# Row-loaded, TensorE-transposed second sequence, joint h transposes and a reordered last sequence in a LayerNorm–FFN kernel

## Chip, cores and metric

One Trainium2 chip, one core. The time is that of one execution on the device, in microseconds.

## What is computed

Eight sequences `b`, each `x[b]` of 256 x 1024 floats with a weight matrix of its own, chosen by `ids[b]`; then a feed-forward network that all share:

```python
y = x[b] @ weight[ids[b]].T                      # 1024 x 1024, fp32
h = layernorm(y) * gamma + beta
a = gelu(fake_quant(h) @ fake_quant(w1).T + b1)  # int8 grid, one scale per row
out[b] = x[b] + fake_quant(a) @ fake_quant(w3).T + b3
```

## The kernel before

Every engine has a program written out by hand; they meet only in semaphores, and each engine and each DMA queue works strictly in its order. All loads and stores are issued by SP.

**One sequence** is two token tiles (t = 0, 1) of 128. Its fp32 product is made from parts: x and weight are transposed, ScalarE (ACT) copies each transposed tile from PSUM as the high part (`split_first`, `split_w`, `split_x`), VectorE (DVE) subtracts to get the low part (`low_first`, `low_w`; GpSimd (POOL) does `low_x`), and TensorE (PE) adds hi·hi, hi·lo and lo·hi. The product has four units (output half kh times contraction half ch) of two pieces; `piece(b, u, k)` is 12 matmuls of 512 columns (L1011 to L1038). The first sequence is loaded on 128 partitions and transposed on PE against an identity, 8 fp32 transposes of 128x128 per step, in the order of the list `FIRST` (`transpose_first`, L1088). Sequences 1 to 7 are loaded in four DMAs of 32 partitions each (`load_unit`, L264; `load_x`, L277) and transposed on DVE in 32x32 blocks (`transpose_w`, L756; `transpose_x`, L772).

**The network** per sequence: ACT copies y (`copy_y`), DVE takes statistics, POOL makes the normalisers and applies gamma and beta (`scale_and_shift`, L417), DVE finds the row scale, ACT rounds (`round_h`), PE transposes h (`transpose_h`, L1047), ACT takes it (`take_h`, L571), PE multiplies by w1 (`ffn1`), DVE rescales (`rescale1`), POOL adds b1, ACT takes Gelu, and the same with w3 (`ffn2`); ACT scales (`scale_ffn2`) and POOL finishes (`finish`, L425): one multiplication by a row of scales and the addition of x + b3. Both h tiles pass through the same PSUM bank, so that the second transpose waits for `rescale1` of the first tile:

```python
if t == 1:
    pe.wait_ge(ffn1_scaled, KH * (TT * f + 1))
...
transpose_tile(h_r[:, t, :], f_ps[:, 0], h_transposed)
```

w1 and w3 come as 16 row tiles; each is loaded (`load_prep`), maxed on DVE (`max_prep`), scaled in four groups (`scales_prep`), rounded on POOL (`round_prep`), transposed on PE (`prepare`) and taken by ACT (`take_prep`), all of it between the pieces of the first two sequences. Two of the slots they are loaded into first hold gamma and beta; `load_prep` of tile 4 or 5 therefore waits until POOL has broadcast these rows (`rows_ready`, L316).

**The order.** After the start (L1206 to L1253 on PE) a loop runs five times (`period(p)`, p = 2 to 6): the FFN of sequence p-1 lies between the pieces of p and p+1. SP's loop (L334) ends with

```python
store(p - 1, 0)
load_unit(p + 2, 1)
store(p - 1, 1)
```

so the load of a unit stands behind a store that waits for POOL's `finish(p-1, 0)`. POOL's loop (L455) is low_x, add_b1, residual (both tiles of x + b3), normalisers, low_x, add_b1, four gamma and beta steps, then `finish` of both tiles. The last sequence has code of its own (`last_period`): DVE takes part of gamma and beta (L875), the FFNs of the last two sequences are woven by hand, and POOL adds b3 to the last x (L506).

## Time and profile before

| | us |
|---|---|
| median of 3 runs (lowest, highest) | 389.77 (389.49, 391.45) |
| the profiled execution | 390.59 |
| its span | 388.7 |
| PE busy | 336.1 (86%) |
| DVE busy | 287.2 (74%) |
| POOL busy | 278.2 (72%) |
| ACT busy | 230.0 (59%) |

PE's busy share is a mean over three stretches: the start to about 131 us, the loop to about 330 us, and the end. A matmul's shown duration is longer than its distance to the next, because matmuls are pipelined; distances between starts are what counts.

### The profile page before, as it was taken

Reading aid. Unit: us, or ns where it says so; the run is one execution under the profiler, and the core shown is the slowest. Engines: PE = TensorE matmul, PEld = TensorE weight load, DVE = VectorE, ACT = ScalarE, POOL = GpSimd, SP = SyncE. Lnnn points to the kernel's source line nnn. Section 1 sums busy time; section 2 is a strip of 40 time slices with the busy share of each in tenths; the row PEclk is TensorE's granted clock in tenths of the full one; section 3 lists DMA queues with packets and bytes.
Section 4 is the critical chain, followed back from the end, with each engine's and each line's share of the span. In section 5 each row is a group of like instructions: output and inputs, shape, how many; then the busy total and the mean of one; then the engine's idle time right before and its main releaser. Section 6 shows DMA issues by size and latency. Waiting matters only on the chain.

```text
span 388.7 us, 5553 instructions
## 1 busy us (share of the span) xinstructions
PE 336.1 (86%) x1732; PEld 227.5 (59%) x1760; DVE 287.2 (74%) x345; ACT 230.0 (59%) x241; POOL 278.2 (72%) x170
## 2 busy tenths in 40 slices
PE   2998816898788999999999999998999999997591
PEld 2786604666565666656665666565656666853240
DVE  1388539766797987788868886888688868388635
ACT  2244519653698747774777567756874777336460
POOL 1404329648559859995999599958996899778563
PEclk9999965999899999999999999999999999999897
DMA  7999998559549799829981999099909900440014
GB/s 251 369 259 332 188 203 197 147 113 208 164 100 217 180 272 219 160 75 293 222 166 57 286 220 192 37 291 217 208 3 287 235 18 0 160 166 1 0 56 162
DMA packets 49946, 67.33 MB, mean 173 GB/s; under 512 B 3078, under 2 KB 43014, under 8 KB 49930
## 3 DMA queue, kind: packets, MB, share of 16 engines
q1 hardware_dynamic: 49930, 67.14, 70.2%
q8 instruction: 8, 0.13, 0.1%
q14 instruction: 8, 0.07, 0.1%
HBM read 58.74 MB, written 8.39 MB: 173 GB/s over the span
## 4 chain that ended last, share of the span: by engine, by line
POOL 38%; issue 16%; PE 8%; DVE 6%; ACT 2%; POOLq 0%; ACTq 0%
POOL x_lo L446 7%; POOL y L421 7%; POOL o L429 6%; POOL x_res L437 6%; POOL a L441 4%; POOL y L423 4%; POOL o L432 3%; PE f_ps L1069 3%; PE t_ps L1069 1%; POOL rstd L407 1%; PE a_ps L1018 1%; DVE x_t L929 1%; PE a_ps L1019 1%; PE a_ps L1020 1%; DVE y L881 1%
## 5 line engine op out<-in xcount | busy, mean ns | idle before, releaser
L1018 PE MATMUL a_ps<-w_hi,x_hi 128*128 128x512 f32 x256 | 109.6, 428 | 2.0 <-ACT y L552 1.2
L1020 PE MATMUL a_ps<-w_hi,x_lo 128*128 128x512 f32 x256 | 101.8, 398 | 0.0
L1019 PE MATMUL a_ps<-w_lo,x_hi 128*128 128x512 f32 x256 | 101.8, 398 | 0.0
L1069 PE MATMUL f_ps<-w_q,q_t 128*128 128x512 bf16 x375 | 88.8, 380 | 5.7 <-ACT q_t L586 3.1
L763 DVE STREAM_TRANSPOSE t_ps<-w_nat 128x1024 f32<-128x1024 f32 x56 | 67.5, 1239 | 20.9 <-DMA w_nat<-in_L_cond_weight 20.6
L537 ACT ACTIVATE w_hi<-t_ps 128x1024 fp32r<-128x1024 f32 x56 | 57.2, 1023 | 31.4 <-DVE t_ps L763 30.3
L769 DVE TENSOR_TENSOR w_lo<-t_ps,w_hi 128x1024 fp32r<-128x1024 f32 x56 | 66.8, 1217 | 9.5 <-ACT w_hi L537 9.3
L1069 PEld LDWEIGHTS f_ps<-w_q,q_t 128*128 128x128 bf16 x400 | 37.1, 98 | 52.4 <-ACT q_t L586 6.4
L1018 PEld LDWEIGHTS a_ps<-w_hi,x_hi 128*128 128x128 f32 x256 | 49.6, 194 | 15.9 <-ACT y L552 3.1
L1020 PEld LDWEIGHTS a_ps<-w_hi,x_lo 128*128 128x128 f32 x256 | 49.2, 192 | 11.2
L1019 PEld LDWEIGHTS a_ps<-w_lo,x_hi 128*128 128x128 f32 x256 | 49.6, 194 | 9.1
L446 POOL TENSOR_TENSOR x_lo<-x_t,x_hi 128x1024 fp32r<-128x1024 f32 x14 | 33.6, 2401 | 22.1 <-ACT x_hi L543 21.9
L441 POOL TENSOR_TENSOR a<-a,rows 128x1024 f32<-128x1024 f32 x14 | 34.5, 2461 | 15.1 <-DVE a L836 15.0
L429 POOL TENSOR_TENSOR o<-o,w_scale_row 128x1024 f32<-128x1024 f32 x14 | 33.3, 2377 | 11.1 <-ACT o L591 11.1
L437 POOL TENSOR_TENSOR x_res<-x_res,rows 128x1024 f32<-128x1024 f32 x14 | 33.8, 2434 | 3.9 <-DMA x_res<-in_x 3.9
L432 POOL TENSOR_TENSOR o<-o,x_res 128x1024 f32<-128x1024 f32 x14 | 33.7, 2409 | 1.1
L423 POOL TENSOR_TENSOR y<-y,rows 128x1024 f32<-128x1024 f32 x12 | 28.7, 2396 | 0.9
L421 POOL TENSOR_TENSOR y<-y,rows 128x1024 f32<-128x1024 f32 x12 | 28.6, 2380 | 0.0
L812 DVE TENSOR_REDUCE g_max<-a 128x1 f32<-128x1024 f32 x14 | 17.0, 1213 | 13.0 <-ACT a L577 13.0
L581 ACT ACTIVATE a<-a,magic,g_inv 128x1024 f32<-128x1024 f32 x14 | 17.4, 1243 | 12.2 <-DVE g_inv L800 12.2
L804 DVE TENSOR_REDUCE h_max<-y 128x1 f32<-128x1024 f32 x14 | 17.0, 1217 | 9.3 <-POOL y L423 9.3
L543 ACT ACTIVATE x_hi<-x_t 128x1024 fp32r<-128x1024 f32 x14 | 14.7, 1052 | 15.2 <-DVE x_t L778 13.4
(143 smaller groups left out, 456.1 us busy)
## 6 DMA issues: line engine op xcount, KB each, us to landing
w_nat<-in_L_cond_weight SPq DMA_DIRECT2D x112, 256.0 KB, 6.6
x_nat<-in_x SPq DMA_DIRECT2D x28, 256.0 KB, 9.9
x_res<-in_x SPq DMA_DIRECT2D x7, 1024.0 KB, 7.0
out<-o SPq DMA_DIRECT2D x14, 512.0 KB, 2.9
w_nat<-in_L_cond_weight SPq DMA_DIRECT2D x4, 512.0 KB, 7.0
w_q<-in_L_ffn_w SPq DMA_DIRECT2D x4, 512.0 KB, 9.1
w_scale_row<-in_L_ffn_w SPq DMA_DIRECT2D x3, 512.0 KB, 13.4
o<-in_x SPq DMA_DIRECT2D x2, 512.0 KB, 4.5
```

What stands on the lines that cost most here:

```text
L421: pool.tensor_tensor(row, row, gamma_row, ALU.mult).then_inc(gamma_done, 1)
L429: pool.tensor_tensor(o[:, t, :], o[:, t, :], w_scale_row[:, 1, :], ALU.mult).then_inc(out_scaled, 1)
L437: pool.tensor_tensor(x_res[:, t, :], x_res[:, t, :], b3_row, ALU.add).then_inc(x_b3_ready, 1)
L441: pool.tensor_tensor(a[:, t, :], a[:, t, :], b1_row, ALU.add).then_inc(ffn1_biased, 1)
L446: pool.tensor_tensor(x_lo[:, half], x_t[:, half], x_hi[:, half].bitcast(F32), ALU.subtract).then_inc(x_lo_ready, 1)
L537: act.activation(part_of_unit(w_hi, u, k), piece_bank(k), ACT.Copy).then_inc(w_hi_ready, 1)
L763: dve.transpose(piece_bank(k).rearrange("p c (kb s) -> p kb c s", s=BLK), w_nat[:, u % 2].rearrange("p kb (c r) -> p kb c r", r=BLK)[:, :, ...
L769: dve.tensor_tensor(part_of_unit(w_lo, u, k), piece_bank(k), part_of_unit(w_hi, u, k).bitcast(F32), ALU.subtract).then_inc(w_lo_ready, 1)
L1018: pe.matmul(ps, hi, w_hi[:, u, c], start=begin, stop=False)
L1019: pe.matmul(ps, hi, w_lo[:, u, c], start=False, stop=False)
L1020: last = pe.matmul(ps, lo, w_hi[:, u, c], start=False, stop=end)
L1069: last = pe.matmul(ps[:, half, :], q[:, c, :], w[:, c, half_of(half)], start=c == 0, stop=c == CB - 1)
```

## The change

The second sequence (b = 1) is no longer loaded in 32-partition DMAs: its weights come as eight row tiles of 128 x 1024 (items 5 to 12 of `FIRST`) and its x as item 13, both on 128 partitions and transposed on PE by ten more steps of `FIRST`; the DVE transposes and `low_x` of b = 1 go. The order of loads, of roundings and of all engines' start is rewritten. PE issues 28 and 12 small matmuls on the bf16 identity before the first two steps. Both h tiles are transposed one behind the other into two banks, and ACT takes them in one instruction. In the last period ACT's two `scale_ffn2` and POOL's two multiplications become four half-tile instructions on DVE, b3 is added to the last x on DVE instead of POOL, the last x is loaded earlier, and DVE's order is new. The core of the diff follows; in the starts of DVE and PE only the new order is shown, and the lines taken out are left out:

```diff
+    FIRST = (((0, 0), (1, 0), (1, 1), (0, 1), (2, 0), (2, 1), (3, 0), (3, 1), (4, 0), (4, 1))
+             + ((5, 0), (6, 0), (7, 0), (8, 0), (13, 0), (13, 1), (9, 0), (10, 0), (11, 0), (12, 0)))
+    FIRST_BUF = (0, 1, 2, 0, 1, 2, 0, 1, 0, 1) + (0, 1) * 5
...
+        w_rows = [buf.rearrange("p k j -> p (k j)").rearrange("p (i d) -> p i d", d=D)[:, i]
+                  for buf in (w_nat[:, 0], w_nat[:, 1], h_r[:], w_nat[:, 0]) for i in range(2)]
...
+                if item > UNITS:
+
+                    kh, tile = divmod(item - 1 - UNITS, RB)
+                    by_block = banks.rearrange("p b (c n) -> p b c n", n=P)
+                    hi, lo = (w[:, CH * kh:CH * (kh + 1), :, tile * P:(tile + 1) * P] for w in (w_hi, w_lo))
+                    return by_block, hi, lo
...
+                    sp.wait_ge(first_transposed, first_piece((12, 8)[u], 0) + 1)
...
+            def load_second_x():
+                for k in range(CH):
+                    sp.dma_start(x_last[:, :, half_of(k)], x[1, :, half_of(k)].rearrange("(t p) j -> p t j", p=P)
+                                 ).then_inc(first_loaded[first_piece(13, k)], 16)
...
+            def load_rows_of_w(tiles):
+
+                adapter = sp.value_load(ids_sb[0:1, 1:2], min_val=0, max_val=N_ADAPTERS - 1)
+                for i in tiles:
+                    sp.wait_ge(first_transposed, first_piece(*((1, 1), (1, 1), (2, 1), (2, 1), (4, 1), (4, 1), (5, 0), (6, 0))[i]) + 1)
+                    src = weight[bass.ds(adapter, 1), i * P:(i + 1) * P, :].rearrange("o p j -> p (o j)")
+                    sp.dma_start(w_rows[i], src).then_inc(first_loaded[first_piece(1 + UNITS + i, 0)], 16)
...
+                else:
+                    sp.wait_ge(x_transposed, LAST - 1)
+                    sp.dma_start(x_last, x[LAST].rearrange("(t p) d -> p t d", p=P)).then_inc(x_last_loaded, 16)
...
-            load_first_x()
+            load_first_x((0,))
             sp.wait_ge(ids_loaded, 16)
             load_first_unit(0)
+            load_first_x((1,))
             load_first_unit(1)
             load_rows()
             load_first_unit(2)
+            load_prep((2, 4))
+            load_rows_of_w((0,))
             load_prep((0,))
+            load_first_unit(3, (1,))
+            load_prep((1,))
             load_first_unit(3, (0,))
-            load_prep((1, 2, 5, 3))
-            load_x(1)
-            load_first_unit(3, (1,))
-            load_prep((7, 4, 12, 8, 6))
-            load_unit(1, 1)
-            load_prep((9,))
-            load_unit(1, 0)
-            load_prep((10,))
+            load_prep((3, 5))
+            load_rows_of_w((1,))
+            load_prep((6,))
+            load_rows_of_w((2, 5))
+            load_second_x()
+            load_prep((11,))
+            load_rows_of_w((3,))
+            load_prep((7, 8, 9))
+            load_rows_of_w((4, 6, 7))
+            load_prep((12, 10))
+            load_unit(2, 1)
             load_x(2)
-            load_prep((11, 13))
-            load_unit(1, 2)
-            load_prep((14,))
-            load_unit(1, 3)
-            load_prep((15,))
-            load_unit(2, 1)
             load_unit(2, 0)
+            load_prep((15, 14))
+            load_unit(2, 2)
+            load_prep((13,))
+            load_unit(2, 3)
             load_residual(0)
-            load_unit(2, 2)
-            load_unit(2, 3)
...
+            round_prep((0, 1, 2, 3, 4, 5, 6))
             normalisers_of(0)
-            round_prep((7, 8))
+            round_prep((7,))
             scale_and_shift(0, 0)
+            round_prep((8,))
             scale_and_shift(0, 1)
-            low_x(1, 1)
+            round_prep((9, 10, 11, 12))
+            low_x(2, 0)
             add_b1(0, 0)
-            round_prep((9, 10, 11, 12))
             add_b1(0, 1)
-            round_prep((13, 14, 15))
+            round_prep((13,))
+            low_x(2, 1)
+            round_prep((14, 15))
+            normalisers_of(1)
             residual(0)
...
-            def residual_last(t):
-                pool.wait_ge(x_last_loaded, 16)
-                pool.tensor_tensor(x_last[:, t], x_last[:, t], b3_row, ALU.add).then_inc(x_last_ready, 1)
-
             f = LAST - 1
             pool.wait_ge(mean_var_ready, TT * LAST + 1)
             pool.wait_ge(normed, TT * LAST)
             normalisers(LAST, slice(0, 1))
-            residual_last(0)
             pool.wait_ge(mean_var_ready, TT * LAST + 2)
             normalisers(LAST + 1, slice(1, 2))
             add_b1(f, 0)
-            residual_last(1)
             add_b1(f, 1)
             pool.wait_ge(ffn1_scaled, KH * (TT * LAST + 1))
             pool.tensor_tensor(a_last[:, 0], a_last[:, 0], b1_row, ALU.add).then_inc(ffn1_biased, 1)
             residual(f)
             for t in range(TT):
-                finish(f, t)
+                pool.wait_ge(last_o_scaled, KH * (t + 1))
+                pool.wait_ge(x_b3_ready, TT * f + t + 1)
+                pool.tensor_tensor(o[:, t, :], o[:, t, :], x_res[:, t, :], ALU.add).then_inc(out_ready, 1)
...
+            def take_h(f):
+
+                act.wait_ge(h_transposed, TT * (f + 1))
+                act.activation(q_t[:].rearrange("p t c k -> p (t c k)"),
+                               f_ps[:].bitcast(I16).rearrange("p h n -> p (h n)"), ACT.Copy).then_inc(h_t_ready, 1)
...
-                take_h(p - 1, 0)
+                take_h(p - 1)
                 split_x(p + 1, 0)
                 both(p + 1, 1)
-                take_h(p - 1, 1)
...
-                scale_ffn2(f, 0, a_ps[:])
+                take(g_transposed, TT * LAST + 1, t_ps[:, 1, 0], q_last[:, 1, 0], g_t_ready)
                 act.wait_ge(g_inv_ready, TT * LAST + 2)
                 act.activation(a_last[:, 1], a_last[:, 1], ACT.Identity, scale=g_inv[:, TT + 1:TT + 2], bias=magic[:]
                                ).then_inc(g_rounded, 1)
-                take(g_transposed, TT * LAST + 1, t_ps[:, 1, 0], q_last[:, 1, 0], g_t_ready)
                 take(g_transposed, TT * LAST + 2, f_ps[:, 0], q_last[:, 1, 1], g_t_ready)
-                scale_ffn2(f, 1, t_ps[:, 0])
...
+                def rescale1_half(f, t, half, ps, dst, col):
+                    dve.wait_ge(ffn1_done, KH * (TT * f + t) + half + 1)
+                    dve.scalar_tensor_tensor(dst[:, t, half_of(half)], ps[:, half, :], h_scale[:, col:col + 1],
+                                             w_scale_row[:, 0, half_of(half)], ALU.mult, ALU.mult
+                                             ).then_inc(ffn1_scaled, 1)
+
+                def finish_half(t, half, ps):
+
+                    dve.wait_ge(ffn2_done, KH * (TT * f + t) + half + 1)
+                    dve.wait_ge(stored[t], 16 * f)
+                    dve.scalar_tensor_tensor(o[:, t, half_of(half)], ps[:, half, :], g_scale[:, t:t + 1],
+                                             w_scale_row[:, 1, half_of(half)], ALU.mult, ALU.mult
+                                             ).then_inc(last_o_scaled, 1)
...
+                for t in range(TT):
+                    residual_last(t)
                 last_statistics(0)
-                last_h(0)
+                last_gamma(0)
+                last_beta(0)
+                scales_h(LAST, 0, TT)
                 last_statistics(1)
-                rescale1(f, 0)
-                last_h(1)
-                rescale1(f, 1, t_ps[:, 0])
+                last_gamma(1)
+                rescale1_half(f, 0, 0, f_ps, a, 0)
+                last_beta(1)
+                rescale1_half(f, 0, 1, f_ps, a, 0)
+                scales_h(LAST, 1, TT + 1)
+                for half in range(KH):
+                    rescale1_half(f, 1, half, t_ps[:, 0], a, 1)
+                rescale1_half(LAST, 0, 0, t_ps[:, 1], a_last, TT)
                 scales_g(f, 0, a[:, 0, :], 0)
-                rescale1(LAST, 0, t_ps[:, 1], a_last, TT)
+                rescale1_half(LAST, 0, 1, t_ps[:, 1], a_last, TT)
+                scales_g(f, 1, a[:, 1, :], 1)
                 rescale_and_bias_half(0)
                 rescale_and_bias_half(1)
-                scales_g(f, 1, a[:, 1, :], 1)
+                scales_g(LAST, 0, a_last[:, 0], TT)
                 max_half(0)
-                scales_g(LAST, 0, a_last[:, 0], TT)
                 max_half(1)
...
+                for t in range(TT):
+                    for half in range(KH):
+                        finish_half(t, half, (a_ps[:], t_ps[:, 0])[t])
...
             low_first(0)
             low_first(1)
             low_first(2)
             low_first(3)
             low_first(4)
             low_first(5)
             low_first(6)
+            max_prep((0, 1))
+            low_first(7)
             max_prep((2, 3))
+            low_first(8)
+            low_first(9)
             scales_prep(0)
+            max_prep((4,))
+            low_first(10)
+            max_prep((5, 6))
+            low_first(11)
+            low_first(12)
+            max_prep((7, 8))
+            low_first(13)
+            low_first(14)
+            scales_prep(1)
             statistics(0, 0)
             statistics(0, 1)
+            low_first(15)
             mean_and_variance(0)
+            low_first(16)
+            max_prep((9, 10, 11, 12))
+            scales_prep(2)
+            low_first(17)
             scales_h(0, 0, 0)
+            low_first(18)
+            transpose_x(2)
+            low_first(19)
             scales_h(0, 1, 1)
+            both(transpose_w, 2, 0)
+            low_w(2, 0, 0)
+            transpose_w(2, 1, 0)
+            statistics(1, 0)
+            low_w(2, 0, 1)
+            low_w(2, 1, 0)
             rescale1(0, 0)
+            transpose_w(2, 1, 1)
+            transpose_w(2, 2, 0)
             max_prep((13, 14))
             rescale1(0, 1)
             max_prep((15,))
             scales_prep(3)
+            low_w(2, 1, 1)
             scales_g(0, 0, a[:, 0, :], 0)
             statistics(1, 1)
             mean_and_variance(1)
+            transpose_w(2, 2, 1)
+            low_w(2, 2, 0)
             scales_g(0, 1, a[:, 1, :], 1)
             transpose_w(2, 3, 0)
             low_w(2, 2, 1)
             transpose_w(2, 3, 1)
+            scales_h(1, 0, 0)
+            both(low_w, 2, 3)
             scales_h(1, 1, 1)
             statistics(2, 0)
...
-                if t == 1:
-                    pe.wait_ge(ffn1_scaled, KH * (TT * f + 1))
-                elif isinstance(f, int) and f == 0:
+                if isinstance(f, int) and f == 0:
                     pe.wait_ge(scale_row_ready, 1)
                 else:
                     pe.wait_ge(ffn2_scaled, TT * f)
-                transpose_tile(h_r[:, t, :], f_ps[:, 0], h_transposed)
+                transpose_tile(h_r[:, t, :], f_ps[:, t], h_transposed)
...
-                pe.wait_ge(h_t_ready, TT * f + t + 1)
+                if t == 0:
+                    pe.wait_ge(h_t_ready, f + 1)
+                else:
+                    pe.wait_ge(ffn1_scaled, KH * (TT * f + 1))
...
+            def warm(count):
+
+                for _ in range(count):
+                    pe.matmul(a_ps[:, 0, 0:P], ident_16[:], ident_16[:], start=True, stop=True)
+
             def transpose_first(j):
                 item, k = FIRST[j]
+                if j < 2:
+                    warm((28, 12)[j])
...
+                if UNITS < item < 13:
+                    for c in range(CB):
+                        dst = banks[:, c // CU, c % CU]
+                        last = pe.transpose(dst, w_rows[item - 1 - UNITS][:, c * P:(c + 1) * P], ident[:])
+                    last.then_inc(first_transposed, 1)
...
+                transpose_h(p - 1, 1)
                 piece(p, 2, 1)
                 ffn1(p - 1, 0)
                 piece(p, 3, 0)
-                transpose_h(p - 1, 1)
...
                 unit(2, 0)
                 transpose_h(f, 0)
+                transpose_h(f, 1)
                 unit(3, 0)
-                pe.wait_ge(h_rounded, TT * f + 2)
-                transpose_tile(h_r[:, 1, :], t_ps[:, 1, 0], h_transposed)
                 unit(2, 1)
                 unit(3, 1)
                 ffn1(f, 0)
+                product_half(q_t[:, 1], w_q[0], t_ps[:, 0], 0, ffn1_done)
                 pe.wait_ge(h_rounded, TT * LAST + 1)
                 pe.wait_ge(y_copied, UNITS * LAST + TT + 1)
                 transpose_tile(h_r[:, 0, :], a_ps[:, 0], h_transposed)
-                pe.wait_ge(h_t_ready, TT * f + 2)
-                product(q_t[:, 1], w_q[0], t_ps[:, 0], ffn1_done)
-                pe.wait_ge(h_t_ready, TT * LAST + 1)
+                product_half(q_t[:, 1], w_q[0], t_ps[:, 0], 1, ffn1_done)
+                pe.wait_ge(h_t_ready, LAST + 1)
...
             piece(0, 2, 0)
+            transpose_first(10)
+            piece(0, 2, 1)
+            transpose_first(11)
+            transpose_first(12)
             prepare((0,))
+            piece(0, 3, 0)
+            transpose_first(13)
+            transpose_first(14)
             prepare((1, 2))
             piece(0, 3, 1)
+            transpose_first(15)
+            transpose_first(16)
+            prepare((3,))
             piece(1, 0, 0)
+            prepare((4, 5))
+            piece(1, 0, 1)
+            transpose_first(17)
+            prepare((6,))
+            piece(1, 1, 0)
+            transpose_first(18)
+            transpose_first(19)
+            prepare((7, 8))
+            piece(1, 1, 1)
             scale_row(0)
+            piece(1, 2, 0)
             transpose_h(0, 0)
+            transpose_h(0, 1)
+            piece(1, 2, 1)
             ffn1(0, 0)
+            piece(1, 3, 0)
             ffn1(0, 1)
             piece(1, 3, 1)
+            prepare((9, 10))
+            piece(2, 0, 0)
+            prepare((11,))
+            piece(2, 0, 1)
+            prepare((12, 13))
+            piece(2, 1, 0)
+            prepare((14, 15))
+            piece(2, 1, 1)
             scale_row(1)
             transpose_g(0, 0)
             ffn2(0, 0)
             transpose_g(0, 1)
             ffn2(0, 1)
```

## Rows read from the trace of the kernel before

**Rows 1.** Busy time by stretch; last columns: PE clock, DMA share, GB/s
```profile
10.00:20.00 10.00, 9.34 (x42) 7.87 (x41) 3.67 (x3) 2.76 (x3) 4.79 (x4) 1.00 1.07 371
...
40.00:50.00 10.00, 8.05 (x60) 6.30 (x59) 4.93 (x7) 5.00 (x6) 4.86 (x4) 1.00 1.10 196
50.00:60.00 10.00, 1.61 (x16) 1.20 (x16) 5.51 (x8) 3.10 (x4) 2.46 (x6) 0.59 1.11 204
```

**Rows 2.** Timeline, first 23 us: start, duration, engine, operation, idle before
```profile
9.01 1.97 PE L1105 MATMUL t_ps<-ident,w_nat 128*128 128x128 f32 x8 [1.71 <-DMA w_nat<-in_L_cond_weight]
...
12.07 1.23 DVE L754 TENSOR_TENSOR w_lo<-t_ps,w_hi 128x1024 fp32r<-128x1024 f32 x1 [2.46 <-ACT w_hi L532]
...
13.11 2.48 POOL L481 PARTITION_BROADCAST rows<-y  x2 [11.01 <-DMA x_t<-in_L_ffn_b]
...
13.35 0.80 PE L1018 MATMUL a_ps<-w_hi,x_hi 128*128 128x512 f32 x1 [0.67 <-DVE w_lo L754]
...
18.21 1.03 PE L1105 MATMUL t_ps<-ident,o 128*128 128x128 f32 x8
...
19.88 0.47 PE L1018 MATMUL a_ps<-w_hi,x_hi 128*128 128x512 f32 x1
...
22.73 1.03 PE L1105 MATMUL f_ps<-ident,w_nat 128*128 128x128 f32 x8
```

**Rows 3.** Timeline, 50 to 60 us
```profile
55.61 1.26 DVE L763 STREAM_TRANSPOSE t_ps<-w_nat 128x1024 f32<-128x1024 f32 x1 [3.94 <-DMA w_nat<-in_L_cond_weight]
...
58.99 1.01 PE L1044 MATMUL f_ps<-ident,w_scale_row 128*128 128x128 bf16 x8 [8.39 <-ACT w_q L598]
```

**Rows 4.** Timeline, PE near 108 us and POOL near 129 us
```profile
108.07 0.62 PE L1044 MATMUL f_ps<-ident,y_first 128*128 128x128 bf16 x8
...
128.69 2.37 POOL L432 TENSOR_TENSOR o<-o,x_res 128x1024 f32<-128x1024 f32 x1
```

**Rows 5.** Timeline and chain of waits, 208 to 251 us
```profile
208.87 2.38 POOL o L432
...
212.42 1.85 SPq L273 DMA_DIRECT2D w_nat<-in_L_cond_weight  x4
...
219.69 2.39 DVE L763 STREAM_TRANSPOSE t_ps<-w_nat 128x1024 f32<-128x1024 f32 x2 [1.19 <-DMA w_nat<-in_L_cond_weight]
...
223.41 0.62 PE L1044 MATMUL f_ps<-ident,h_r 128*128 128x128 bf16 x8 [0.51 <-DVE a L836]
...
223.43 2.41 POOL L441 TENSOR_TENSOR a<-a,rows 128x1024 f32<-128x1024 f32 x1 [1.29 <-DVE a L836]
...
248.53 2.38 POOL o L432
```

**Rows 6.** Timeline of the last period, 336 us to the end
```profile
336.49 0.69 DVE L870 BATCH_NORM_STATS2 stats<-y 128x6 f32<-128x512 f32 x1 [5.32 <-ACT y L641]
...
347.30 3.25 DVE L881 SCALAR_TENSOR_TENSOR y<-y,rstd,rows 128x1024 f32<-128x1024 f32 x1
...
353.52 0.62 PE L1044 MATMUL a_ps<-ident,h_r 128*128 128x128 bf16 x8 [2.62 <-ACT h_r L568]
...
365.25 0.62 PE L1044 MATMUL t_ps<-ident,a 128*128 128x128 bf16 x8 [3.75 <-ACT a L581]
...
377.17 3.62 PE L1069 MATMUL f_ps<-w_q,w_nat 128*128 128x512 bf16 x16
...
375.26 0.75 DVE L925 SCALAR_TENSOR_TENSOR x_t<-t_ps,g_scale,w_scale_row 128x512 f32<-128x512 f32 x1 [5.21 <-PE t_ps L1069]
...
378.15 2.49 DVE L929 TENSOR_TENSOR x_t<-x_t,x_nat 128x512 f32<-128x512 f32 x1
...
384.09 0.69 DVE L929 TENSOR_TENSOR x_t<-x_t,x_nat 128x512 f32<-128x512 f32 x1
```

**Rows 7.** Groups by line: count, busy time, mean ns of one
```profile
L573 ACT ACTIVATE q_t<-f_ps 128x1024 bf16<-128x1024 int16 x13 | 13.3, 1020 | 7.9 <-PE f_ps L1044 7.8
...
L452 POOL TENSOR_SCALAR w_q<-w_q,wq_inv,magic 128x1024 f32<-128x1024 f32 x4 | 4.7, 1200 | 13.1 <-DVE wq_inv L800 13.1
```

More of the change, by code:

```diff
@@ L291, in load_residual, with load_first_x @@
                 sp.dma_start(x_res[:], src).then_inc(x_res_loaded, 16)
-            def load_first_x():
-                for half in range(CH):
+            def load_first_x(halves):
+                for half in halves:
                     cols = half_of(half)
-                    sp.dma_start(x_first[:, :, cols], x[0, :, cols].rearrange("(t p) j -> p t j", p=P)
+                    sp.dma_start(o[:, :, cols], x[0, :, cols].rearrange("(t p) j -> p t j", p=P)
                                  ).then_inc(first_loaded[first_piece(0, half)], 16)
@@ L999, in _ @@
             transpose_w(2, 3, 1)
+            scales_h(1, 0, 0)
+            both(low_w, 2, 3)
             scales_h(1, 1, 1)
-            both(low_w, 2, 3)
             statistics(2, 0)
```

216 lines of the change are left out of this document (83 added, 133 removed).

## The prediction

> **What bounds the kernel now.** I read the busy time by stretch, then the timeline of PE at the start, then the waits of one turn of the loop, then the last period.
>
> The reader is to see three kernels in one. In the start PE is kept waiting. DMA moves 371 GB/s while whole-width loads are under way and 196 GB/s when the 32-partition loads of sequence 1 are, with the engines equally full (share 1.07 and 1.10), and from 50 to 60 us PE works 1.6 of 10 us [rows 1]. The gap's end shows whom it waits for: DVE stands 3.94 us for a weight unit that it gets at 55.61, ACT's in-order queue stands behind DVE, and PE starts again at 58.99 after 8.39 us, at half clock: 8 transposes take 1.01 us instead of 0.62 [rows 3, 4].
>
> In the loop PE looks like the bound, but it isn't. Follow one turn [rows 5]: POOL ends `finish` of tile 0 at 208.87 + 2.38 = 211.25; SP, whose queue held the store that waits for it, issues the next unit at 212.42; DVE gets it at 219.69, two transposes, then `rescale1`; POOL starts `add_b1` at 223.43 and has no gap to speak of until it ends `finish` again at 248.53 + 2.38 = 250.91. The turn is 39.66 us, 27.5 of it POOL's own work and 12.2 the way over SP, DMA and DVE. PE is not in this circle, and waits 0.51 us in it for the h transpose. I take the circle for the bound of the five turns.
>
> In the last period latencies bound: PE idles 2.62 and 3.75 us before two transposes, and after its last product (377.17 + 3.4) DVE still needs until 384.78 [rows 6].
>
> **Prices.** A warm piece is 22.73 - 19.88 = 2.85 us, a cold one 18.21 - 13.35 = 4.86; a transposing step on PE is (19.88 - 18.21)/2 = 0.84 [rows 2]. One w tile on PE is 0.5, that is 0.62 less the overlap with what follows [rows 4], rounding on POOL 1.2 [rows 7], a whole-tile POOL step 2.4 [rows 4], a low part on DVE 1.2 and a maximum, over as many columns, the same [rows 2], an FFN product 3.4 [rows 6].
>
> **Part 1, the first 14 us.** Half of x (0.52 MB) now follows the first weights: 0.52/0.371 = 1.4 us earlier for the load that PE waits for at 9.01 [rows 1, 2]. Warm-up: if it raises the clock, 8 transposes take 0.84 instead of 1.97 and the piece 2.85 instead of 4.86, 3.1 us together; if not, 0. The 40 small matmuls (about 0.11 each at half clock, from 8 in 1.01 us [rows 3]) fit ahead of the two loads, so they cost at most the 1.3 us of the second group. I take 3.1, since all of PE's idle time there is filled. First piece ends at 18.2 - 4.5 = 13.7.
>
> **Part 2, to the end of sequence 1's product.** I walk PE's new order with these prices and check each step against its load. Added: ten PE steps, 8.4 us, no longer hidden by anything. Removed: eight DVE transposes and one of x, some 12 us of DVE, and two POOL steps. The weak point on SP: w tile 4 is now third from the rows, and waits for two broadcasts of POOL, 13.11 + 2.48 = 15.6 [rows 2], with all later loads queued behind. From then, with 2 us until data flow, at 371 GB/s and 1.5 us for sharing: w3's first half after 3.15 MB at 27.6 (PE wants it at 26.4, a stall of 1.2); weight row tile 3 after 8.39 MB at 41.7 (wanted at 40.9, a stall of 0.8); the last row tile and w tile 10 after 12.6 MB at 53, before they are wanted. DVE's queue then holds the next gate: the transpose of x of sequence 2 stands ahead of the last low part, and that x comes on 32 partitions behind a unit: 53 + 2.1/0.196 + 1.5 = 65.2, plus 2.4 and 1.2 = 68.8, where PE arrives at 66.8. From there one piece, both h transposes (1), a piece, `ffn1`, a piece, `ffn1`, a piece: 68.8 + 4 x 2.85 + 1 + 6.8 = 88. Before, this point is 108.07 [rows 4]. Gain 20.
>
> What these 371 GB/s rest on is one stretch. The Trainium skill (SBUF — State Buffer, Door 1: The DMA port swizzle) says that partitions 0 to 31 reach half of the ports, with 189 GB/s against 328 for all 128 at 1 MiB. The trace agrees with the ratio. By the page's 328 the last row tile would land 4.4 us later and the total be some 3 us higher than mine.
>
> **Part 3, to the loop.** The gain is not kept whole, since the circle is entered by POOL. After sequence 1's product POOL still has two roundings, normalisers (done about 9.4 us after the product, behind DVE's `scales_g` and statistics), residual 4.8, gamma and beta 9.6, `finish` 4.8: 28.6. Before it took 128.69 + 2.37 - 108.07 = 23.0 [rows 4], because the residual lay earlier. So `finish` of tile 0 ends at 88 + 28.6 = 116.6 instead of 131.1: gain 14.5. PE itself is ready for the loop at about 116, so nothing is added by it; its two g transposes and products at the end now have no pieces between them, some 4 us of bare latency, and hide under POOL.
>
> **Part 4, the loop.** The joint h transpose removes PE's wait of 0.51 us (`ffn1` of tile 1 waits for `rescale1` instead, a piece later, long done). ACT's take grows from 1.02 [rows 7] to about 1.9 and is ahead of `split_x`, whose x isn't ready before. Neither is in the circle: 0. Bounds: 5 x 0.9 slower, if the longer take comes through; 5 x 0.7 faster, if PE was the bound. I take 0.
>
> **Part 5, the end.** The late beta step took 3.25 us where 1.3 is normal, beside POOL [rows 6]; its order ahead of POOL's `add_b1` and the two b3 additions leaving POOL remove PE's 2.62. `scales_g` of the second tile moves ahead of the bias halves and removes most of 3.75; late is next the take of its transposes, behind three Gelus on ACT, a new wait of some 1.9. PE came back from the 3.75 us at low clock, another 1.5. Together 5.5 to 6. After the last product, DVE's additions took 2.49 us where 0.69 is normal [rows 6], twice, beside POOL's last two steps; POOL now has half the work and is done before: 2.5. The four new halves on DVE are of the kind that takes 0.75, 3 us together, and fall in the 5.21 in which it waits for w3's products [rows 6]. Sum 8; bounds 4 and 10.
>
> Here a rule speaks against a part of it. A DVE step with two SBUF inputs and a POOL step exclude each other for a whole instruction, says the Trainium skill (SBUF — State Buffer, SBUF: two separate sides). The two b3 additions on DVE would then stand behind POOL's `finish`, up to 2.4 us each. By the trace DVE idles 5.32 us there [rows 6], so by row and rule alike the sum changes only if they spill over, by at most 2.
>
> **Sum.** 14.5 + 0 + 8 = 22.5 on the profiled execution's 390.59 (1.9 beyond its span): 368.1. The median of the runs is 0.8 lower: 367.3.
>
> **Rivals.**
> - *PE is the loop's bound.* For: its wait in a turn is as short as half a us [rows 5]. Against: the circle above, whose steps are each released by the last. Then also 5 x 0.7: 363.8. Chance 0.13.
> - *Loads come late.* Mixed queues run at the mean of the two rates, 283 GB/s: the 14.7 MB up to sequence 2's x land at 71, 6 us later than above, and the tail gives 5 instead of 8: 376. For: every load shares, and SP's queue has new waits in it. Chance 0.22.
> - *Slower.* Loading on 128 partitions is no faster, because the DMA engines, full in both stretches, are the limit: at 196 GB/s sequence 2's x lands at 17.6 + 75 + 1.5 = 94, the last low part is at 98 instead of 69, and 29 us more than eat the 22.5: 396. It decides below some 215 GB/s. Against it stands the 371. Chance 0.03.
> - A start that gives nothing beyond its added 8.4 us and an end that gives 4 would be within 0.5%: 0.02.
>
> My forecast has 0.60. The range takes in fast starts with the first rival (358) and late loads with a poor end (379). A measurement here tells 0.5% from no change. Faster 0.95, same 0.02, slower 0.03.
>
> **What would show it.** PE's first piece at 0.23 us a matmul from about 10.8; no gap at 50 to 60 us; DMA at over 330 GB/s from 18 to 50 us; sequence 1's product done near 88; POOL's first `finish` near 117; turns still 39.7 us long, with PE waiting elsewhere; last product ending near 360, the span under 6 us after. Turns of 39 us or less refute the circle; DVE waiting for x_nat over 3 us means the late-load rival.

## Result and profile after

The changed kernel takes 372.27 us (median of 4 runs, 369.72 to 374.43) beside 390.20 before on the same chip: ratio 0.9535, 95% interval 0.9465 to 0.9605. The same file in a second series gave 370.07, ratio 0.9466 [0.9414, 0.9518]. The forecast, 367.3, has the right sign, and the result lies in its range, but it promises some 3 to 5 us too much.

The profiled execution took 374.43 us (span 372.5), before 390.59 (388.7). The gain is 16.2 us where I forecast 22.5. Three marks divide both traces: the end of POOL's first and sixth `finish` of a tile 0 (the loop's entry and exit) and the end of the span. The last column is the second profile of the changed kernel (371.4 us, span 369.5), from the second series.

| stretch | before | after | change | forecast | after, second profile |
|---|---|---|---|---|---|
| to the end of the first `finish` | 131.06 | 121.71 | -9.35 | -14.5 | 117.85 |
| five turns | 199.78 | 200.35 | +0.57 | 0 | 202.88 |
| from there to the end of the span | 57.86 | 50.44 | -7.42 | -8 | 48.77 |

The page of the changed kernel: PE is now 92% busy, and the hole at a seventh of the span is gone.

```profile
PE 341.4 (92%) x1854; PEld 235.9 (63%) x1880; DVE 285.5 (77%) x344; ACT 227.1 (61%) x232; POOL 263.4 (71%) x164
...
PE   6898899996976999999999999999899989999885
...
POOL 1402259841998579995999599968997699946831
PEclk9999999999899999999999999999999999999989
...
POOL 41%; issue 22%; DMA 13%; DVE 11%; PE 7%; SPq 3%; ACT 2%; POOLq 0%; DVEq 0%
```

**Loads**, busy time by stretch (columns as in [rows 1]). 196 and 204 GB/s have become 345 to 412, at nearly the same share of the engines (0.98 to 1.05, before 1.10 and 1.11); only where the loads on 32 partitions begin again, from 50 us, does the rate fall back.

```profile
10.00:20.00 10.00, 8.83 (x52) 7.52 (x53) 4.81 (x4) 3.92 (x4) 4.80 (x4) 1.00 1.05 345
...
30.00:40.00 10.00, 10.00 (x68) 8.81 (x67) 9.79 (x11) 4.61 (x5) 4.78 (x4) 1.00 0.98 354
40.00:50.00 10.00, 8.74 (x62) 7.39 (x62) 6.73 (x8) 6.08 (x8) 0.00 (x0) 1.00 1.03 412
50.00:60.00 10.00, 10.00 (x78) 8.68 (x77) 8.70 (x13) 8.12 (x10) 8.80 (x10) 1.00 1.10 210
```

**PE's first 15 us**, timeline, against [rows 2]: the first transposes still take 1.91 us, the ones behind the second warm-up 1.10, and the first piece lasts from 12.26 to 15.12. That this is the clock is read from the durations alone: the column of the granted clock shows 1.00 in all of the first 15 us, in the kernel before too.

```profile
2.17 3.17 PE L1159 MATMUL a_ps<-ident 128*128 128x128 bf16 x28 [2.17 <-POOL ident L513]
5.13 1.91 PE L1186 MATMUL t_ps<-ident,o 128*128 128x128 f32 x8
6.83 1.18 PE L1159 MATMUL a_ps<-ident 128*128 128x128 bf16 x12
8.79 1.10 PE L1186 MATMUL t_ps<-ident,w_nat 128*128 128x128 f32 x8 [0.78 <-DMA w_nat<-in_L_cond_weight]
...
12.26 0.50 PE L1080 MATMUL a_ps<-w_hi,x_hi 128*128 128x512 f32 x1 [1.02 <-DVE w_lo L794]
...
15.12 1.04 PE L1186 MATMUL t_ps<-ident,o 128*128 128x128 f32 x8
```

**From sequence 1's product to the loop**, timeline of DVE, PE and POOL, against [rows 4]. The product ends at 88.76 (3.13 before 91.89, where PE resumes); the forecast said 88. What follows is new: DVE waits for a weight unit, then for w tile 13; `rescale1` of tile 1 stands behind both, and PE's w tiles 9 and 10 wait for it.

```profile
85.27 1.26 DVE L803 STREAM_TRANSPOSE t_ps<-w_nat 128x1024 f32<-128x1024 f32 x1 [2.38 <-DMA w_nat<-in_L_cond_weight]
88.08 1.22 DVE L861 TENSOR_REDUCE wq_max<-w_scale_row 128x1 f32<-128x1024 f32 x1 [1.56 <-DMA w_scale_row<-in_L_ffn_w]
...
90.35 1.40 DVE L876 SCALAR_TENSOR_TENSOR a<-f_ps,h_scale,w_scale_row 128x512 f32<-128x512 f32 x2
...
91.89 1.05 PE L1111 MATMUL f_ps<-ident,x_res 128*128 128x128 bf16 x16 [3.13 <-DVE a L876]
...
110.06 0.61 PE L1111 MATMUL f_ps<-ident,a 128*128 128x128 bf16 x8 [1.16 <-issue]
112.29 3.40 PE L1134 MATMUL f_ps<-w_q,q_t 128*128 128x512 bf16 x15 [1.62 <-ACT q_t L627]
116.98 0.61 PE L1111 MATMUL f_ps<-ident,a 128*128 128x128 bf16 x8 [1.30 <-ACT o L632]
118.71 3.63 PE L1134 MATMUL f_ps<-w_q,q_t 128*128 128x512 bf16 x16 [1.12 <-ACT q_t L627]
...
100.41 0.22 POOL L441 TENSOR_TENSOR var_eps<-mean_var,eps 128x2 f32<-128x2 f32 x1
...
116.92 2.35 POOL L466 TENSOR_TENSOR o<-o,w_scale_row 128x1024 f32<-128x1024 f32 x1 [0.92 <-ACT o L632]
```

**One turn of the loop**, timeline, against [rows 5]: the same circle, step for step (POOL ends `finish` at 202.14, the unit's load is issued behind the store at 203.30, DVE has it at 210.58, POOL starts `add_b1` at 214.32), while PE waits at another place (0.39 ahead of an FFN2 product).

```profile
197.36 3.63 PE L1134 MATMUL f_ps<-w_q,q_t 128*128 128x512 bf16 x15 [0.39 <-ACT q_t L627]
199.75 2.39 POOL L469 TENSOR_TENSOR o<-o,x_res 128x1024 f32<-128x1024 f32 x1
202.16 0.37 SPq L359 DMA_DIRECT2D out<-o  x1
203.30 1.84 SPq L285 DMA_DIRECT2D w_nat<-in_L_cond_weight  x4
...
210.58 2.39 DVE L803 STREAM_TRANSPOSE t_ps<-w_nat 128x1024 f32<-128x1024 f32 x2 [1.20 <-DMA w_nat<-in_L_cond_weight]
214.32 2.42 POOL L478 TENSOR_TENSOR a<-a,rows 128x1024 f32<-128x1024 f32 x1 [1.29 <-DVE a L876]
```

**The end**, timeline, against [rows 6]. Of 2.62 and 3.75 us, 0.41 and nothing are left; a new wait of 2.74 with eight matmuls at a fallen clock behind it (3.29 instead of 1.89; granted 0.56 from 355.37 to 358.40) takes part of it back. From the start of the last product to the end of the span it is 7.64 us, before 11.53. The last additions take 0.69 instead of 2.49.

```profile
322.31 6.74 DVE L917 TENSOR_TENSOR x_nat<-x_nat,rows 128x1024 f32<-128x1024 f32 x2
...
342.49 0.62 PE L1111 MATMUL a_ps<-ident,h_r 128*128 128x128 bf16 x8 [0.41 <-ACT h_r L607]
...
350.30 0.61 PE L1111 MATMUL t_ps<-ident,a 128*128 128x128 bf16 x8
...
355.37 3.29 PE L1134 MATMUL t_ps<-w_q,q_t 128*128 128x512 bf16 x8 [2.74 <-ACT q_t L685]
...
364.86 3.62 PE L1134 MATMUL f_ps<-w_q,w_nat 128*128 128x512 bf16 x16
...
369.30 0.69 DVE L1000 TENSOR_TENSOR x_t<-x_t,x_nat 128x512 f32<-128x512 f32 x1
```

### The profile page after: what moved, and what is told of

Same layout as the page of the kernel before. It is cut to its first block, busy times and chain, and to the rows that moved or that the text cites. A ratio compares the mean times of both kernels' runs of the same rounds, so it can differ in the third digit from the quotient of the medians.

```text
span 372.5 us, 5769 instructions
## 1 busy us (share of the span) xinstructions
PE 341.4 (92%) x1854; PEld 235.9 (63%) x1880; DVE 285.5 (77%) x344; ACT 227.1 (61%) x232; POOL 263.4 (71%) x164
## 3 DMA queue, kind: packets, MB, share of 16 engines
q1 hardware_dynamic: 46186, 67.14, 68.8%
## 4 chain that ended last, share of the span: by engine, by line
POOL 41%; issue 22%; DMA 13%; DVE 11%; PE 7%; SPq 3%; ACT 2%; POOLq 0%; DVEq 0%
POOL y L458 8%; POOL x_res L474 7%; POOL o L466 6%; POOL y L460 5%; DMA x_res<-in_L_ffn_w 5%; POOL a L478 4%; POOL x_lo L483 4%; POOL o L469 3%; DMA w_scale_row<-in_L_ffn_w 3%; PE t_ps L1134 2%; DMA h_r<-in_L_cond_weight 2%; DVE x_nat L917 2%; DMA x_t<-in_L_ffn_b 2%; DVE wq_max L861 2%; DMA w_nat<-in_L_cond_weight 2%
## 5 line engine op out<-in xcount | busy, mean ns | idle before, releaser
L1080 PE MATMUL a_ps<-w_hi,x_hi 128*128 128x512 f32 x256 | 107.5, 420 | 2.4 <-DVE w_lo L794 1.2
L803 DVE STREAM_TRANSPOSE t_ps<-w_nat 128x1024 f32<-128x1024 f32 x48 | 57.5, 1238 | 11.7 <-DMA w_nat<-in_L_cond_weight 11.5
L809 DVE TENSOR_TENSOR w_lo<-t_ps,w_hi 128x1024 fp32r<-128x1024 f32 x48 | 57.2, 1219 | 8.9 <-ACT w_hi L574 8.7
L574 ACT ACTIVATE w_hi<-t_ps 128x1024 fp32r<-128x1024 f32 x48 | 49.0, 1023 | 21.9 <-DVE t_ps L803 21.1
L1080 PEld LDWEIGHTS a_ps<-w_hi,x_hi 128*128 128x128 f32 x256 | 48.5, 189 | 15.7 <-ACT y L589 3.2
L478 POOL TENSOR_TENSOR a<-a,rows 128x1024 f32<-128x1024 f32 x14 | 33.4, 2385 | 19.7 <-DVE a L876 17.5
L483 POOL TENSOR_TENSOR x_lo<-x_t,x_hi 128x1024 fp32r<-128x1024 f32 x12 | 28.7, 2395 | 20.8 <-ACT x_hi L580 20.8
L466 POOL TENSOR_TENSOR o<-o,w_scale_row 128x1024 f32<-128x1024 f32 x12 | 28.5, 2379 | 3.7 <-ACT o L632 3.7
L469 POOL TENSOR_TENSOR o<-o,x_res 128x1024 f32<-128x1024 f32 x12 | 29.6, 2465 | 0.9
L458 POOL TENSOR_TENSOR y<-y,rows 128x1024 f32<-128x1024 f32 x12 | 28.6, 2382 | 0.0
L618 ACT ACTIVATE a<-a 128x1024 f32<-128x1024 f32 x14 | 14.8, 1056 | 16.4 <-POOL a L478 16.4
L569 ACT ACTIVATE w_hi<-t_ps 128x1024 fp32r<-128x1024 f32 x14 | 14.2, 1027 | 17.1 <-PE t_ps L1173 11.0
```

Of the source, the lines that this page charges most:

```text
L458: pool.tensor_tensor(row, row, gamma_row, ALU.mult).then_inc(gamma_done, 1)
L466: pool.tensor_tensor(o[:, t, :], o[:, t, :], w_scale_row[:, 1, :], ALU.mult).then_inc(out_scaled, 1)
L478: pool.tensor_tensor(a[:, t, :], a[:, t, :], b1_row, ALU.add).then_inc(ffn1_biased, 1)
L574: act.activation(part_of_unit(w_hi, u, k), piece_bank(k), ACT.Copy).then_inc(w_hi_ready, 1)
L803: dve.transpose(piece_bank(k).rearrange("p c (kb s) -> p kb c s", s=BLK), w_nat[:, u % 2].rearrange("p kb (c r) -> p kb c r", r=BLK)[:, :, ...
L809: dve.tensor_tensor(part_of_unit(w_lo, u, k), piece_bank(k), part_of_unit(w_hi, u, k).bitcast(F32), ALU.subtract).then_inc(w_lo_ready, 1)
```

## Experiments

Three questions: does the circle over SP's store set the loop, which part of the change earned what, and why did the start give up to 5 us less. Ratios are to the kernel before on the same chip.

### The changed kernel again, and the warm-up

No edit in the first; in the second `warm((28, 12)[j])` is `warm((0, 0)[j])`.

> The changed kernel once more, as the measure for the others of this chip. 370 to 374 us (ratio to before near 0.953). Every theory expects turns of the loop near 39.7 us and the same wait of DVE for w tile 13 near 87 us; if that wait were chance, it would be missing here.

> The changed kernel without the 40 small matmuls on the identity. My theory: the first steps and the first piece run at half clock again, so the first piece ends 3 us later (about 18 instead of 15.1 us); but PE then waits for w loads at 28 us and near 43 us, so that 1 to 2 us of it are given back: total +1 to +2 us. Rival (the clock's gain is kept whole): +3 us. Rival (loads set the start): 0.

Measured: 370.07, 0.9466 [0.9414, 0.9518], and without the warm-up 370.58, 0.9454 [0.939, 0.9519]. The medians are 0.5 us apart and each interval reaches 2 to 2.5 us to either side, so that neither my theory (1 to 2 us) nor the rival (0) is decided, and the whole 3 us lie at the edge of what the intervals allow. The timeline of PE without it shows the local loss: three groups of transposes at 1.91 to 1.97 us and a piece that ends at 18.9 instead of 15.1.

```profile
5.20 1.94 PE L1186 MATMUL t_ps<-ident,o 128*128 128x128 f32 x8 [5.20 <-DMA o<-in_x]
9.34 1.97 PE L1186 MATMUL t_ps<-ident,w_nat 128*128 128x128 f32 x8 [2.21 <-DMA w_nat<-in_L_cond_weight]
11.11 1.91 PE L1186 MATMUL f_ps<-ident,w_nat 128*128 128x128 f32 x8
13.68 0.79 PE L1080 MATMUL a_ps<-w_hi,x_hi 128*128 128x512 f32 x1 [0.67 <-DVE w_lo L794]
...
18.91 1.03 PE L1186 MATMUL t_ps<-ident,o 128*128 128x128 f32 x8
```

Behind it PE no longer meets its load waits (1.3 and 0.8 us between 15 and 90 us in the profile with the warm-up, none in the one without). So part of the lead is waited away where the loads set the pace: of 3.8 us at the first piece, 1.3 are left at the end of sequence 1's product (88.3 and 89.5) and at the first `finish` (117.85 and 119.10).

The repeat also shows how far the start moves from one execution to the next: DVE's two waits at 85 and 88 us are 1.18 and 0.56 here instead of 2.38 and 1.56, and the first `finish` ends at 117.85 instead of 121.71. But FFN2 of tile 1 took 5.93 us, at a granted clock of 0.58 (from 115.25 to 120.80), instead of 3.63; POOL's `finish` of tile 1 waits 4.57 us for it instead of 1.86, and of the lead of 3.9 us only 1.2 are left there (127.30 and 128.47). Timeline of PE and POOL in the repeat:

```profile
107.46 3.63 PE L1134 MATMUL f_ps<-w_q,q_t 128*128 128x512 bf16 x16 [1.39 <-ACT q_t L627]
...
122.42 2.39 POOL L466 TENSOR_TENSOR o<-o,w_scale_row 128x1024 f32<-128x1024 f32 x1 [4.57 <-ACT o L632]
```

The end of the first `finish` is thus a mark that can show more than the start has earned.

### The load ahead of the store

On SP, on the changed kernel, in the loop (shown) and for the one such pair ahead of it:

```diff
-                store(p - 1, 0)
                 if not (isinstance(p, int) and p + 2 > LAST):
                     load_unit(p + 2, 1)
+                store(p - 1, 0)
                 store(p - 1, 1)
```

> The changed kernel with the load of unit 1 issued ahead of the store of tile 0, in the loop and once ahead of it. If the circle POOL's finish, SP's store, load, DVE, rescale, POOL bounds the loop, this cuts it: turns fall from 39.7 to 38.3 to 38.8 us (PE's own work), and the total by 5 to 7 us. If PE bounds the loop, turns stay within 0.2 us and the total is the same.

Measured: 361.45, 0.9252 [0.9201, 0.9304], 2.1 points or 8.4 us below the changed kernel's 0.9466, somewhat more than the 5 to 7 that I expected. The profiled execution took 366.27 us. The windows from the second `finish` to the sixth, four turns, first of the changed kernel and then of this one, show it: PE has the same work, 153 us; only its idle time goes, 6.4 to 0.8.

```profile
162.57:322.06 159.49, 153.12 (x756) 101.69 (x771) 128.76 (x157) 107.32 (x109) 137.18 (x72) 1.00 0.74 178
```

```profile
160.39:313.99 153.60, 152.79 (x772) 101.77 (x771) 128.63 (x157) 108.29 (x109) 137.31 (x72) 1.00 0.76 178
```

In the timeline SP issues both stores one behind the other, with the unit's load issued ahead of them (at 193.25), and `add_b1` of POOL starts with no idle time:

```profile
196.37 2.37 POOL L469 TENSOR_TENSOR o<-o,x_res 128x1024 f32<-128x1024 f32 x1
198.77 5.57 SPq L359 DMA_DIRECT2D out<-o  x2
...
209.61 2.41 POOL L478 TENSOR_TENSOR a<-a,rows 128x1024 f32<-128x1024 f32 x1
```

So the circle bound the loop, at 40.0 us a turn before and 40.1 and 40.6 in the two profiles of the changed kernel (means of five), and PE bounds it at 38.4 to 38.5 on this kernel once it is cut. The profile of the first combination below, of an execution of 361.28 us, has 38.6.

### Joint h transposes and load first, each alone and together, on the kernel before

The first edit in the loop alone: `transpose_h(p - 1, 1)` is moved behind `transpose_h(p - 1, 0)` into the second bank of `f_ps`, ACT takes both in one copy. The second is the swap of above. The third has both.

> The kernel before, with the two h tiles transposed at once in the five turns of the loop and nothing else of the change. The circle theory (POOL's finish, SP's store, the load behind it, DVE's transpose, the rescaling, POOL's b1, finish) says that the loop's turn of 39.7 us stays: time within 1 us of before (389.8 to 391.5), and FFN2 waits for the second g tile or the scaling of o instead. The theory that PE's wait ahead of the second h transpose [rows 5] was on the path says 0.5 to 0.7 us a turn, 3 us faster (387 to 388).

> The kernel before, with SP issuing the load of the next unit ahead of the store of the first output tile instead of behind it; h tiles still transposed one by one. Circle theory: the turn falls from 39.7 us until another chain binds, most likely PE with its wait for the second h transpose, which the change would take away: 38.7 to 39.2 a turn, 3 to 6 us faster than before. If the one-by-one transposes cost nothing even with the circle cut, the turn falls to 38.4 as it did in the changed kernel, 8 to 9 us faster. If the store was no part of what bounded it: no difference.

> Both edits on the kernel before. Circle theory: turn 38.4 us as in the changed kernel with the load first, so 5.5 turns of 1.3 us = 7 to 8.5 us faster than before, and 2 to 3.5 us faster than with the load first alone (that difference is what the joint transposes are worth once the circle is cut). Rival, that they are worth nothing in either setting: the same as the load first alone.

| kernel | median us | ratio [95%] | mean turn of five | PE busy in four turns |
|---|---|---|---|---|
| joint h | 389.83 | 1.0 [0.9968, 1.0031] | 40.12 | 154.04 of 160.38 |
| load first | 380.65 | 0.9768 [0.9727, 0.9809] | 38.51 | 152.96 of 153.51 |
| both | 382.77 | 0.9775 [0.9724, 0.9826] | 38.66 | 153.11 of 154.45 |

The ratios are the recorded ones; the plain quotients of the medians are 0.977 for the load first and 0.982 for both. The joint transpose alone is worth nothing, as the circle says, and by neither figure does it add to the load first. That PE's wait ahead of the second h transpose would cost 2 to 3.5 us once the circle is cut was wrong: with the load first it is not there. The list of waits of "load first" between 200 and 300 us has only this for PE:

```profile
PE a_ps L1018 <- ACT y L552: 0.5, 3, 0.2
```

The wait of 0.51 us in [rows 5] was itself a shadow of the circle: the h transpose waited for `rescale1`, and `rescale1` for the late weight unit.

### The start: w tile 13

SP loads w tile 13 ahead of units 2 and 3 of sequence 2, and DVE takes the maxima of tiles 13 to 15 and does `rescale1` of tile 1 ahead of the transposition of unit 2.

> The changed kernel with w tile 13 loaded ahead of tiles 15, 14 and of unit 2 of sequence 2, and DVE's maxima of 13 to 15 and the rescaling of the second tile ahead of that unit's transpose. If the start loses its last 4 to 5 us because DVE's queue stands behind tile 13, PE's wait of 3.1 us near 89 us goes, POOL's first finish ends 3 to 4 us earlier than 121.7, and the total falls by 3 us. Rival (POOL's own work and the two uncovered FFN products set the entry to the loop): less than 1 us.

Measured: 371.53, 0.9493 [0.9437, 0.955]: no gain. The timeline of PE shows the wait of 3.13 gone; another has taken half its place, and at the end of the start FFN2 of tile 0 stands alone, at a fallen clock:

```profile
91.28 0.47 PE L1078 MATMUL a_ps<-w_hi,x_hi 128*128 128x512 f32 x1 [1.46 <-ACT y L588]
...
106.98 0.61 PE L1109 MATMUL f_ps<-ident,a 128*128 128x128 bf16 x8 [1.16 <-issue]
108.98 5.21 PE L1132 MATMUL f_ps<-w_q,q_t 128*128 128x512 bf16 x16 [1.39 <-ACT q_t L626]
```

The fallen clock is a granted 0.66 from 108.98 to 113.80. POOL's normalisers came at 97.81 instead of 100.41, but `finish` waited 2.04 us for ACT's scaled output and ended at 120.20: of 2.6 us, 1.5 came through. Beside the repeat of the same series (a wait of 0.54 instead of 3.13, normalisers at 97.36, `finish` at 117.85) even that is no gain.

### The end: which engine finishes sequence 6

`finish_half` on DVE is taken out; ACT's `scale_ffn2` and POOL's `finish` stand in its place, as in the kernel before.

> The changed kernel with one part of the last period put back: the last outputs of sequence 6 are scaled by ACT from PSUM and multiplied and finished by POOL, as in the kernel before, instead of DVE's four halves straight from PSUM. Theory that this part carries the gain of the end: 2 to 3 us slower than the changed kernel (372 to 374 beside 370 to 371). Rival, that the end's chain runs through sequence 7's h, g and FFN2 on PE and DVE alone and sequence 6's output is beside it: within 0.7 us, and the gain of the end then lies in sequence 7's order.

Measured: 374.62, 0.9602 [0.9556, 0.9648]. From the loop's exit to the end of the span it is 53.64 us, against 50.44 and 48.77 in the two profiles of the changed kernel. The profile with 48.77 is the one to compare with: in both the clock does not fall behind the wait of 2.74 (the eight matmuls take 1.90). PE starts its last product 41.11 us after the exit here and 41.14 there, so that all of the 4.9 us lie behind it. DVE's last additions of sequence 7 again run beside POOL, and the timeline prices that; the rows of the changed kernel above have 0.69:

```profile
360.72 2.06 DVE L997 TENSOR_TENSOR x_t<-x_t,x_nat 128x512 f32<-128x512 f32 x1
...
363.48 2.05 DVE L997 TENSOR_TENSOR x_t<-x_t,x_nat 128x512 f32<-128x512 f32 x1
```

So this part is worth 4.9 us of the end by the profiles, and 5.3 by the ratios (0.9602 and 0.9466), where I expected 2 to 3. The profile has another use: its start met almost no wait for w tile 13 (0.74 us for the unit, none for the tile), and its first `finish` ended at 116.42.

### The end: the copy behind the half Gelus

```diff
+                take(g_transposed, TT * f + 2, t_ps[:, 0, 0], q_t[:, 1], g_t_ready)
                 for half in range(KH):
...
-                take(g_transposed, TT * f + 2, t_ps[:, 0, 0], q_t[:, 1], g_t_ready)
```

> The changed kernel with one instruction of the last period moved on ACT: the copy of sequence 6's second transposed g tile out of PSUM now stands ahead of the two half Gelus of sequence 7 instead of behind them. Theory: PE's wait of 2.74 us at 355.37 is the wait for that copy, which stands behind a half Gelu that itself waits 2.13 us for DVE; it goes, and with it the half clock of the eight matmuls behind it (3.29 us instead of 1.89); PE waits some 1.5 us for the transposition of the next g tile instead. 1.5 to 3 us faster than the changed kernel: 367.5 to 369.5. Rival, that the end hangs on DVE's last g scales (done at 356.85) and not on this copy: within 0.7 us of the changed kernel.

Measured: 368.47, 0.9459 [0.9411, 0.9508], beside 0.9466 for the changed kernel: nothing that can be told. The wait of 2.74 is gone, and PE waits at the next g transpose instead:

```profile
352.95 0.62 PE L1111 MATMUL t_ps<-ident,w_nat 128*128 128x128 bf16 x8 [2.24 <-ACT w_nat L707]
```

The rounding that it waits for hangs on DVE's scales of sequence 7. The end is 48.28 us long, against 48.77 where the 2.74 brought no fall of the clock. The other profiles agree: without a fall 48.30 with the early copy, with a fall 50.04 and 50.01 with it and 50.35 to 50.51 without. The copy is worth the 0.5 us by which the wait is shorter, and the fall, some 1.7 us, came with either order. My theory took the nearest wait for the bound.

### Combinations

On the changed kernel: load first and the early copy; with w tile 13 added; and with that, tile 1's half of piece (2, 1, 1) moved between the first g transposes and their FFN2, ACT taking w tiles 14 and 15 ahead of a normalisation.

> The changed kernel with the load ahead of the store and the ACT copy moved. The two act in different stretches (loop and end), so they should add up: 361.5 less 1.5 to 3 = 358.5 to 360. If the end's gain is not real, 361 to 362.

> As the run before, and w tile 13 loaded and its maximum taken earlier in the start (the edit that gave nothing by itself while the circle through the store set the loop). With the circle cut PE bounds the loop without a wait, so each microsecond that PE idles in the start now counts: its wait of 4.46 us for the rescaling at 90.89 falls to about 1.5. 1.5 to 3 us faster than the run before (356 to 358.5). Rival, that another wait takes its place, as without the load first: within 0.7 us of it.

> As the run before, and at the end of the start half a piece of sequence 2's product is put between the first g transposes and their FFN2 (ACT takes w tiles 14 and 15 ahead of a normalisation for it). It covers the wait of 1.39 us ahead of that FFN2, and with that should keep PE at the full clock in it (5.2 us with the fall, 3.6 without). 1 to 3 us faster than the run before if PE's idle time in the start is the bound; nothing if the normalisation put back makes POOL late instead.

Measured: 362.57, 0.93 [0.9258, 0.9342]; 363.50, 0.9321 [0.928, 0.9361]; 364.94, 0.9358 [0.9325, 0.9391]. None of the additions gained on the load first alone (0.9252), and the last is 1.1 points behind it, outside both intervals. Two expectations of mine took a wait of one profile for a fixed cost: the 4.46 us before w tile 9 (PE's transposes of it), in the profile of the load-first kernel, is absent from that of the first of these, with the start unchanged; and the fall of the clock in FFN2 of tile 0 (5.2 us), which the third was to remove, is absent from the profile of the second (3.63). The third covers the FFN2, and the timeline of PE shows waits for ACT and the fallen clock one tile on:

```profile
106.74 0.61 PE L1109 MATMUL f_ps<-ident,a 128*128 128x128 bf16 x8 [2.06 <-issue]
108.74 3.63 PE L1132 MATMUL f_ps<-w_q,q_t 128*128 128x512 bf16 x16
114.47 0.61 PE L1109 MATMUL f_ps<-ident,a 128*128 128x128 bf16 x8 [2.10 <-ACT o L631]
116.20 5.03 PE L1132 MATMUL f_ps<-w_q,q_t 128*128 128x512 bf16 x16 [1.12 <-ACT q_t L626]
```

The fastest version measured is the change with the load first: 361.45 us, ratio 0.9252; with the early copy as well it can't be told from it.

## Why the prediction was right, and where it was not

**Part 1, half right.** The warm-up shortened the weights' transposes (1.10 instead of 1.97) and the first piece (2.86 instead of 4.86), not the transposes of x. The load came at 8.79, 0.2 us earlier and not 1.4. First piece at 15.1 instead of 13.7, before 18.2. Without the warm-up the first piece ends 3.8 us later and the first `finish` 1.3 us later: most of the term of 3.1 us is lost again in load waits. What is left of it over the whole is not resolved.

**Part 2, right.** Row loads at 345 to 412 GB/s where I had 371; waits for the first half of sequence 0's weight unit 3 and for row tile 3 of 1.18 and 1.26 us where I had 1.2 and 0.8; product at 88.76 where I had 88. One stall of the walk was not there: I had PE reach the last low part at 66.8 and wait 2.0 us for it until 68.8; it came there 2.4 later and waited 0.21, to start at 69.40. The two errors cancel. The rival by which loads come late, and the one by which 128 partitions bring nothing, fall with these rows. No run has the row loads without the rest of the new start: that they carry its gain is read from the rates and the missing gap, and not shown by an edit. The Trainium skill (SBUF — State Buffer, Door 1: The DMA port swizzle) has 328 GB/s for a load of 1 MiB on all 128 partitions; the trace shows more, 345 to 412 over stretches with several queued, and for the 32-partition loads 196 to 210 where it has 189.

**Part 3, the step that failed.** I let POOL need 28.6 us from the product to the end of `finish`; it took 32.95. I had counted POOL's work and DVE's, and left out what DVE's queue waits for: `rescale1` of tile 1 stands behind a unit's transposition and w tile 13's maximum, whose loads SP issues last. With waits of 2.38 and 1.56 us there, POOL begins the residual 13.0 us after the product (at 101.74) where I had 9.4; the other 0.8 us is `finish`, which waits 0.92 for ACT's scaled output.

In the four profiles where DVE waits 1.2 us or less for the unit and 0.6 or less for the tile (the repeat, no warm-up, `finish` on POOL, the early copy), the residual begins 8.8 to 10.4 us after the product, about as forecast, and the whole takes 29.5 to 29.9, since `finish` waits 0.15 to 1.76 us for ACT. So the sum is 1 us short even where the load is in time. That one of them ended `finish` at 116.42, where I had 116.6, is luck: its product ended at 86.6, 1.4 earlier than my 88. The load is in time in some executions and not in others.

With the tile taken early nothing was gained. The traces suggest why: PE's last two FFN2 products, which I called "some 4 us of bare latency" that "hide under POOL", do not hide. They carry 5.2 us of waits and at times a fall of the clock (3.6 us become 5.0 to 5.9), and `finish` waits for them. That they are what holds the start now is read from the traces; the one edit that was to cover them made new waits, so a gain from it is not shown.

**Part 4, right, and shown.** The joint transpose alone: ratio 1.0 within 0.3%. The store-load circle alone, cut: 2.3 points on the kernel before, 2.1 on the changed one. The rival in which PE bounds the loop describes the kernel after the circle is cut, and even then the joint transposes have nothing to remove. Its bound of 0.7 us a turn was a wait that the circle made. The zero holds for the turn's mechanism and not for each execution: the five turns took 0.57 us more than before in one profile and 3.1 in the other, whose first turn contains the 4.57 us wait for ACT.

**Part 5, right in size, not in its parts.** 7.4 in the first pair of profiles, 9.1 by the second profile, forecast 8. Up to the start of the last product it gave 3.5 (5.2 where the clock did not fall), forecast 5.5 to 6: PE's 2.62 became 0.41, its 3.75 nothing, the new wait 2.74 where I had 1.9. Behind it, it gave 3.9, forecast 2.5; the finishing halves on DVE carry this, for with ACT and POOL in their place the stretch is 4.9 longer. One part too high and one too low make the 8 come out. The two b3 additions behave as the rule of the Trainium skill has it that the prediction weighed (SBUF — State Buffer, SBUF: two separate sides), by which such a DVE step and a POOL step exclude each other: 3.37 us each beside POOL's `finish`, where two halves at 0.69 make 1.4, and POOL's own step 3.25 instead of 2.4. They are 1.4 longer than the idle 5.32 us, but PE shows a wait of only 0.41 in that part.

Together, on the profiled execution: 5.1 us too little at the loop's entry (0.8 from the later product, 4.3 in Part 3), 0.6 in the loop and 0.6 at the end, which is the 6.3 by which 374.43 exceeds my 368.1. The second profile of the changed kernel, 371.4, is off by 3.3, made otherwise: 1.3 at the entry and 3.1 in the loop, less 1.1 at the end.

## What to carry to other kernels

Before pricing a removed wait in a loop, find what made it: if the engine that ends the wait is itself held up by the circle that sets the turn, the wait can be that circle's shadow, as here, where it was worth nothing before the circle was cut and was gone afterwards. A store that waits for the last result of a turn must not stand ahead of the next load in one in-order queue; moving it was worth 8 to 9 us here, nearly half as much as the whole change. When a forecast lets a stage end by an engine's work, go through every instruction queued ahead of its inputs and check its load as well, with the spread of that load between executions.

## What the runs showed of the hardware

A fall of TensorE's clock behind a wait is not a fixed cost: behind the same two waits (1.16 us ahead of the transposes, 1.39 ahead of the product) the same 16 matmuls of FFN2 of tile 0 took 3.63 us in three profiles (granted clock 1.00) and 4.96, 5.07, 5.21, 5.31 and 5.31 in five others (0.65 to 0.70). Loads, too, come at different times for the same program: DVE's wait for one weight unit was 0.44, 0.65, 0.74, 1.18, 2.38 and 4.95 us in six profiles with the same start up to there. They come from several chips, but 1.18 and 4.95 are from one. Gains under 2 us in such a start could not be told apart by their times, and a wait that one profile shows has to be seen in a second one before it is counted.
